# A two-layer transformer on one core: the first attention moves its tokens, outputs are normalised on GpSimd

## The chip, the cores and the metric

One core of one Trainium2 chip. The time is that of the whole launch on the device, in microseconds (us). The engines are named PE (TensorE), PEld (its weight loads), DVE (VectorE), ACT (ScalarE), POOL (GpSimd) and SP (SyncE, here only the queue that issues the DMAs).

## The reference

Two layers over 2048 tokens of width 512, all in fp32. Each layer normalises its input once and adds an attention and a feed-forward of it to the stream.

```python
x = x + attention0(xn) + ffn0(xn)     # 16 heads of 32, block-wise decayed linear attention; top 4 of 16 experts' blocks
xn = layernorm(x)
x = x + attention1(xn) + ffn1(xn)     # 32 heads of 64 over 8 key heads, causal softmax; fp4 weights, silu gate, rms norm
...
h = einsum('nf,ibf->nib', xf, W1b)            # ffn0: 16 blocks of 128 hidden units
h = gelu(h) * mask[:, :, None]
y = einsum('nib,fib->nf', h, W2b)
...
scores = where(causal, einsum('bhqd,bhkd->bhqk', q, kf) / sqrt(64), min)   # attention1
out = einsum('bhqk,bhkd->bhqd', softmax(scores), v)
return out.transpose(0, 2, 1, 3).reshape(b, s, 2048) @ o_w.T
```

## The kernel before

Six stages follow each other, each a block of five engine programs with a barrier at its end: attention0, feed_forward0, projections1, attention1, output1, feed_forward1. Inside a stage the engines are ordered by semaphores alone, written out by hand. All DMAs that matter are issued by SP, in the order of its program. To keep fp32 accuracy, most products are split: each operand is a high part (rounded by ACT) and a low part (the rest, by DVE or GpSimd), and `split_matmul` (lines 50 to 52) makes three matmuls: high by high, high by low, low by high.

**attention0** goes over four chunks of 512 tokens. Its tensors `x`, `xb` and `xn` hold a chunk of tokens, the copy that the output is added to, and the normalised chunk. `xacc` (16 tiles of 128x512), the token stream, is allocated only after this stage.

**feed_forward0** goes over four quarters of four hidden blocks (`q`), in each over four chunks (`c`). For a chunk PE makes four hidden blocks (`HB[b]`, 12 matmuls each), ACT applies gelu, DVE the mask, ACT takes the high part `hT[0]`, GpSimd the low part `hT[1]`, and PE adds the second product into `YB[t]`, 12 matmuls for each of four blocks. In quarters 1 to 3 DVE also unpacks fp4 weights for the last stage between these steps. The first quarter's weights go straight into two rooms of `xacc`, tiles 8 to 15 (`load_first`).

**attention1** has 16 units (key head by sequence) of 24 steps: 16 long ones (queries 512 to 1023) and 8 short ones (queries 0 to 511). In a step PE makes scores (line 1755), DVE the negative maximum (lines 1692, 1695), ACT the exponentials with their sum (line 1662), and DVE transposes them 32 by 32 (lines 1710 to 1715). PE multiplies them with the values in blocks of 32 keys (line 1770) at later steps: `SHORT_VALUES` and `LONG_VALUES` give, for a step counted from the unit's first, the blocks, so that steps from 24 on fall into the next unit. ACT evicts finished halves at the steps of `SHORT_LEFT` and `LONG_LEFT`, and SP stores them to `OT`. At step `INVERT` DVE takes the reciprocals of the sums (line 1721), transposes them (line 1724), and SP writes them to `R`. Within `attention1` GpSimd does nothing.

**output1** goes over 32 steps (2 sequences of 16 pairs of heads). Each loads a row of `OT` into `of` and its reciprocals from `R`, spread over 64 partitions each, into `rd`; DVE multiplies them (line 1921), ACT and GpSimd make the parts (lines 1895, 1902), PE does 24 matmuls. In the first 16 steps a slice of `WoG` is loaded and split too. Row 0, its reciprocals and two slices are loaded ahead at the end of attention1 (`output1_rooms`).

## Time and profile before

| | us |
|---|---|
| median of 3 runs | 2274.7 |
| lowest, highest | 2269.36, 2278.79 |
| profiled execution, its time | 2273.54 |
| its span (first to last instruction) | 2271.8 |
| PE, DVE, ACT, POOL busy in it | 2084.5, 1578.6, 845.8, 366.6 |
| mean granted TensorE clock | 0.964 of 2.4 GHz |

The span is what the rows below count from; the time of the execution is 1.7 us more. PE is busy in 92% of the span, but this share is a mean over stages with different limits.

### The profile page before, as it was taken

How to read it: one execution, taken by the hardware profiler on the slowest of the kernel's cores; microseconds unless marked ns; L12 is line 12 of the kernel's file. 1: busy time of each engine (PE TensorE's matmuls, PEld its weight loads, DVE VectorE, ACT ScalarE, POOL GpSimd, SP SyncE). 2: the span in 40 equal slices, each digit the busy share in tenths (PEclk: the TensorE clock that was granted, in tenths of full speed). 3: DMA queues.
4: the chain of work that ended last, by engine and by line, in shares of the span. 5: the costliest groups of instructions: out<-in, count | busy, mean ns of one | idle time of the engine just before them, and what ended most of it. 6: DMA issues, size and time to landing. Idle time of an engine off the chain costs nothing. (4 is left out here: it accounts for less than half of the span.)

```text
span 2271.8 us, 52890 instructions
## 1 busy us (share of the span) xinstructions
PE 2084.5 (92%) x21680; PEld 1472.5 (65%) x21680; DVE 1578.6 (69%) x2439; ACT 845.8 (37%) x1773; POOL 366.6 (16%) x249
## 2 busy tenths in 40 slices
PE   7999969999998999978998898998988899999998
PEld 5777748887786788734444444444445687787776
DVE  5544323699976345499989999999994462577776
ACT  4322122222223200055555655556553221234443
POOL 0111111323220155400000000000000344221111
PEclk9999989999998999979999999999998899999999
DMA  5122145344427633423333433333332999420101
GB/s 182 57 94 76 38 172 181 102 132 132 125 76 285 184 111 125 150 67 103 100 91 96 116 101 97 104 94 104 110 92 78 286 249 273 141 84 19 56 1 38
DMA packets 205019, 268.18 MB, mean 118 GB/s; under 512 B 42304, under 2 KB 123520, under 8 KB 202112
## 3 DMA queue, kind: packets, MB, share of 16 engines
q1 hardware_dynamic: 203936, 264.85, 38.4%
q8 instruction: 162, 2.65, 0.5%
q14 instruction: 57, 0.47, 0.1%
q10 hardware_dynamic: 864, 0.21, 0.0%
HBM read 181.81 MB, written 83.17 MB: 117 GB/s over the span
## 5 line engine op out<-in xcount | busy, mean ns | idle before, releaser
L1662 ACT ACTIVATE a_prob<-ps,a_nmax 128x256 f32<-128x256 f32 (+7 forms) x512 | 376.7, 738 | 326.9 <-DVE a_nmax L1692 228.7
L1755 PE MATMUL ps<-xacc 64*128 64x512 f32 (+5 forms) x1536 | 389.7, 550 | 80.8 <-ACT a_prob L1662 74.9
L1692 DVE TENSOR_REDUCE a_nmax<-ps 128x1 f32<-128x1024 f32 (+3 forms) x256 | 256.2, 1001 | 45.8 <-PE ps L1755 44.7
L1755 PEld LDWEIGHTS ps<-xacc 64*128 64x128 f32 x1536 | 146.4, 197 | 200.1 <-ACT a_prob L1662 118.4
L1713 DVE STREAM_TRANSPOSE a_pt_long<-a_prob 128x768 f32<-128x768 f32 (+1 forms) x256 | 238.0, 930 | 0.0
L2083 DVE SCALAR_TENSOR_TENSOR f_part<-ps,f_gu_scale,f_part 128x512 f32<-128x512 f32 x264 | 185.2, 746 | 66.9 <-PE ps L2130 53.5
L1770 PE MATMUL ps<-a_pt_long,xacc 32*64 32x256 f32 (+2 forms) x6144 | 211.7, 386 | 1.3 <-ACT a_o L1672 1.3
L1770 PEld LDWEIGHTS ps<-a_pt_long,xacc 32*64 32x64 f32 x6144 | 122.4, 137 | 109.5 <-issue 97.9
L940 POOL TENSOR_TENSOR f_hT_lo<-f_h,f_hT_hi 128x512 fp32r<-128x512 f32 x64 | 93.8, 1474 | 286.4 <-ACT f_hT_hi L923 286.4
L1902 POOL TENSOR_TENSOR o_oT_lo<-xacc,o_oT_hi 128x512 fp32r<-128x512 f32 x2 | 2.9, 1497 | 803.7 <-ACT o_oT_hi L1895 803.7
L1752 PE MATMUL ps<-xacc 64*128 64x128 bf16 x1024 | 113.8, 227 | 5.2 <-ACT a_prob L1662 5.0
L50 PE MATMUL ps<-o_wo_hi,o_oT_hi 128*128 128x512 f32 x256 | 103.2, 403 | 16.6 <-POOL o_oT_lo L1902 16.2
L1695 DVE TENSOR_REDUCE a_nmax<-ps 128x2 f32<-128x1024 f32 (+3 forms) x128 | 105.4, 823 | 17.0 <-PE ps L1755 15.0
L50 PE MATMUL ps<-f_xt_hi,f_w_hi 128*128 x256 | 100.6, 393 | 17.7 <-DMA f_xt_lo<-scratch_xt 17.7
L1710 DVE STREAM_TRANSPOSE a_pt_short<-a_prob 128x512 f32<-128x512 f32 (+3 forms) x256 | 114.1, 484 | 0.0
L1770 PEld LDWEIGHTS ps<-a_pt_short,xacc 32*64 32x64 f32 x3712 | 71.8, 134 | 60.6 <-issue 45.3
L1368 DVE TENSOR_TENSOR k_rp<-ps,k_cosq 128x512 f32<-128x512 f32 x64 | 43.9, 686 | 94.0 <-POOL k_qo L1245 78.7
L919 ACT ACTIVATE f_gl<-ps 128x512 f32<-128x512 f32 x64 | 38.1, 595 | 183.5 <-PE ps L52 183.5
L1245 POOL TENSOR_TENSOR k_qo<-k_rp 128x512 f32<-128x512 f32 x64 | 87.4, 1386 | 102.6 <-DVE k_rp L1368 102.6
L50 PE MATMUL ps<-f_w_hi,f_hT_hi 128*128 128x512 f32 x256 | 101.1, 395 | 2.9 <-POOL f_hT_lo L940 2.4
L51 PE MATMUL ps<-o_wo_lo,o_oT_hi 128*128 128x512 f32 x256 | 101.4, 396 | 0.0
L52 PE MATMUL ps<-o_wo_hi,o_oT_lo 128*128 128x512 f32 x256 | 101.2, 395 | 0.0
(234 smaller groups left out, 4489.7 us busy)
## 6 DMA issues: line engine op xcount, KB each, us to landing
xacc<-scratch_QT SPq DMA_DIRECT2D x512, 64.0 KB, 2.0
scratch_QT<-k_qo SPq DMA_DIRECT2D x64, 256.0 KB, 2.3
xacc<-scratch_V SPq DMA_DIRECT2D x64, 256.0 KB, 4.7
scratch_OT<-a_o SPq DMA_DIRECT2D x32, 512.0 KB, 5.0
o_of<-scratch_OT SPq DMA_DIRECT2D x31, 512.0 KB, 5.2
o_rd<-scratch_R SPq DMA_DIRECT2D x62, 256.0 KB, 8.0
f_block<-in_packed SPq DMA_DIRECT2D x33, 256.0 KB, 3.6
f_mask<-scratch_maskT SPq DMA_DIRECT2D x16, 512.0 KB, 5.1
```

What stands on the lines that cost most here:

```text
L50: pe.matmul(out, lh[lsel], rh[rsel], start=first, stop=False)
L51: pe.matmul(out, lh[lsel], rl[rsel], start=False, stop=False)
L52: return pe.matmul(out, ll[lsel], rh[rsel], start=False, stop=last)
L1662: last = nc.scalar.activation(prob[:, n % PRING, s].rearrange("p (a w) -> p a w", w=w), SC[n % 2][:, a, 0:w], ACT.Exp, bias=nmax[:, n % 4, ...
L1692: nc.vector.tensor_reduce(nmax[:, n % 4, 0:1], SC[n % 2][:, :, 0:width(0, t)], AX.XY, ALU.max, negate=True).then_inc(maxed, 1)
L1695: nc.vector.tensor_reduce(nmax[:, n % 4, :], SC[n % 2][:, :, 0:width(1, t)], AX.X, ALU.max, negate=True).then_inc(maxed, 1)
L1710: last = nc.vector.transpose(pt_short[:, 0:blocks, h, t, :], src)
L1713: last = nc.vector.transpose(pt_long[:, unit % 2, 0:near, h, t - 4, :], src[:, 0:near, :])
L1752: pe.matmul(sc[:, a, w - P:w], identb[r, s, :], causal[r, s, :], start=s == 0, stop=False, skip_group_check=True)
L1755: last = pe.matmul(sc[:, a, 0:w], q[r, slot, heads[a * hf], :], kt[r, b, keys], start=not masked, stop=True, skip_group_check=True)
L1770: last = pe.matmul(out[:, :, a - t0:4, :], v[rows, b, j, :], part[rows, c::2, a - p0:t0 + 4 - p0, :], start=j == 0, stop=j == BLOCKS[hf] - ...
L2083: nc.vector.scalar_tensor_tensor(part[:, s % 2, i, :], PB[(2 * k + i) % 4], gu_scale[:, s % NBK, i, k:k + 1], part[:, s % 2, i, :], ALU.mu ...
```

## The change

It has five parts.

1. `xacc` is allocated before attention0, which keeps `xb`, `xn` and `x` in its tiles 0 to 3, 8 to 11 and 12 to 15. In its last chunk, when `xn` and `x` are used up, SP loads the first quarter's W1T and W2T into their rooms.
2. feed_forward0 begins with four loads: the first and second half of the first chunk's k, high and low part each. PE's first hidden block waits for the halves by themselves (`first_xt`). The first chunk has a loop of its own on PE.
3. In the second product of feed_forward0 PE does, for a hidden block, the eight matmuls with `hT[0]` first (waiting for `h_hi`), and then the four with `hT[1]` (waiting for `h_lo`).
4. In attention1 the short value blocks go in another order over six steps in place of five, their eviction and both stores move by a step, `INVERT` is one step earlier, and each finished half is multiplied with its reciprocals there, by GpSimd for 31 halves and by DVE for the last. The reciprocals come back from `R` by two DMAs a half (`load_inverse`), into one buffer.
5. output1 loads rows already normalised: no `rd`, no multiplication; rows 0 and 1 are loaded ahead.

```diff
@@ attention0, SP
+                    else:
+                        sp.wait_ge(xt_done, KC * NCH)
+                        for dst, src in zip(feed_forward0_rooms(xacc), (d["W1T"][:, 0:C], d["W2T"][0:C, :])):
+                            sp.dma_start(dst, src.rearrange("(k p) n -> p k n", p=P)).then_inc(rest_in, 16)
...
@@ attention0, tensors
-        x = sb("x", [P, TPC, C])
-        xb = sb("xb", [P, TPC, C])
-        xn = sb("xn", [P, TPC, C])
+        xb, xn, x = [xacc[:, r * TPC:(r + 1) * TPC, :] for r in (0, 2, 3)]
...
@@ feed_forward0, SP
-                load_first(0, d["W1T"][:, 0:QC])
+                xt_in.give_credit(sp)
+                for i in range(2):
+                    for s in range(2):
+                        sp.dma_start(xt[s][:, 2 * i:2 * i + 2, 0:CH].bitcast(F32), d["xt"][s][:, 2 * i:2 * i + 2, 0:CH]
+                                     ).then_inc(first_xt[i].sem, 16)
...
-                load_chunk(0)
-                load_first(1, d["W2T"][0:QC, :])
...
@@ feed_forward0, PE
+                                if first and b == 0 and k % 2 == 0:
+                                    pe.wait_ge(first_xt[k // 2].sem, 32)
...
-                            pe.wait_ge(h_lo.sem, h_lo.now(it, b + 1))
+                            pe.wait_ge(h_hi.sem, h_hi.now(it, b + 1))
                             for t in range(TPC):
...
-                                last = split_matmul(pe, YB[t], hT, [w[:, p] for w in w2], b == 0, b == BPQ - 1,
-                                                    np.s_[:, b, t * P:(t + 1) * P], np.s_[:, b, :])
+                                part = hT[0][:, b, t * P:(t + 1) * P]
+                                for s in range(2):
+                                    pe.matmul(YB[t], part, w2[s][:, p, b, :], start=b == 0 and s == 0, stop=False)
+                            pe.wait_ge(h_lo.sem, h_lo.now(it, b + 1))
+                            for t in range(TPC):
+                                last = pe.matmul(YB[t], hT[1][:, b, t * P:(t + 1) * P], w2[0][:, p, b, :],
+                                                 start=False, stop=b == BPQ - 1)
...
@@ attention1
-SHORT_VALUES = {26: range(0, 3), 27: range(3, 6), 28: range(6, 9), 29: range(9, 13), 30: range(13, 16)}
+SHORT_VALUES = {26: (0, 15, 14, 13, 12), 27: (11, 10, 9, 8), 28: (7, 6), 29: (5, 4), 30: (3, 2), 31: (1,)}
...
-SHORT_LEFT = {31: (0,), 32: (1,)}
+SHORT_LEFT = {32: (0, 1)}
...
-SHORT_STORE, LONG_STORE = 34, 50
-INVERT = USTEPS + 2
+SHORT_STORE, LONG_STORE = 35, 51
+SHORT_INVERSE, LONG_INVERSE = 29, 36
+INVERT = USTEPS + 1
...
@@ attention1, SP
-                    sp.wait_ge(evicted, 2 * i + 2)
+                    sp.wait_ge(scaled, i + 1)
...
+                def load_inverse(u, hf):
+                    g, b = divmod(u, NB1)
+                    tok = slice(FIRST[hf] * P, (FIRST[hf] + 4) * P)
+                    sp.wait_ge(r_stored, 64 * (u + 1))
+                    wait(sp, scaled, order(u, hf))
+                    for a in range(2):
+                        sp.dma_start(rd[a * HD1:(a + 1) * HD1, :, :],
+                                     d["R"][g, b, a::2, tok].partition_broadcast(HD1)).then_inc(rd_in, 16)
...
@@ attention1, GpSimd
+                for i in range(2 * NU - 1):
+                    pool.wait_ge(evicted, 2 * i + 2)
+                    pool.wait_ge(rd_in, 32 * (i + 1))
+                    nc.gpsimd.tensor_tensor(o[:, i % 2].rearrange("p s t i q -> p s (t i q)"),
+                                            o[:, i % 2].rearrange("p s t i q -> p s (t i q)"), rd[:], ALU.mult
+                                            ).then_inc(scaled, 1)
...
@@ output1
-                    for a in range(2):
-                        sp.dma_start(rd[a * HD1:(a + 1) * HD1, n % 2, :],
-                                     d["R"][k // 2, b, 2 * (k % 2) + a, :].partition_broadcast(HD1)
-                                     ).then_inc(o_in[n % 3], 16)
...
-                        nc.vector.tensor_tensor(row(n, s), row(n, s), inverse(n, s), ALU.mult).then_inc(scaled, 1)
```

Three places of the order show what moves. The first is SP's queue from the last loads of attention0 to the first of feed_forward0 (`f_xt` is the chunk of normalised tokens, `scratch_x` the output of attention0). Before:

```order
L230 DMA scratch_x<-a_xb 128x512 [waits a0_y_out] x4
L179 UNCONDITIONAL_BRANCH [waits a0_y_stored,a0_mask_stored,a0_xt_stored]
L792 UNCONDITIONAL_BRANCH [waits barrier_Pool_Activation_PE_DVE_SP_release]
L798 DMA xacc<-in_W1T 128x4x512
L809 DMA f_mask<-scratch_maskT 128x4x512
L803 DMA f_xt_hi<-scratch_xt 128x4x512 [waits f0_xt_in]
L803 DMA f_xt_lo<-scratch_xt 128x4x512
L798 DMA xacc<-in_W2T 128x4x512
```

And now:

```order
L227 DMA xacc<-in_W1T 128x4x512 [waits a0_xt_done]
L227 DMA xacc<-in_W2T 128x4x512
L229 DMA scratch_maskT<-a_maskT 16x512 [waits a0_mask_out]
L232 DMA scratch_x<-xacc 128x512 [waits a0_y_out] x4
L177 UNCONDITIONAL_BRANCH [waits a0_y_stored,a0_rest_in,a0_mask_stored,a0_xt_stored]
L800 UNCONDITIONAL_BRANCH [waits barrier_Pool_Activation_PE_DVE_SP_release]
L814 DMA f_xt_hi<-scratch_xt 128x2x512
L814 DMA f_xt_lo<-scratch_xt 128x2x512
L814 DMA f_xt_hi<-scratch_xt 128x2x512
L814 DMA f_xt_lo<-scratch_xt 128x2x512
L818 DMA f_mask<-scratch_maskT 128x4x512
```

Both weight loads stand ahead of the barrier, and the first chunk comes in four loads directly behind it.

The second is PE in feed_forward0, at the start of the second product of a chunk (`f_hT` is the hidden tile, `f_w` the second weights). Before:

```order
L52 MATMUL ps<-f_xt_hi,f_w_lo 128x512
L50 MATMUL ps<-f_w_hi,f_hT_hi 128x512 [waits f0_y_added,f0_h_lo,f0_w_lo]
L51 MATMUL ps<-f_w_lo,f_hT_hi 128x512
L52 MATMUL ps<-f_w_hi,f_hT_lo 128x512
L50 MATMUL ps<-f_w_hi,f_hT_hi 128x512 [waits f0_y_added]
```

And now:

```order
L52 MATMUL ps<-f_xt_hi,f_w_lo 128x512
L1061 MATMUL ps<-f_w_hi,f_hT_hi 128x512 [waits f0_y_added,f0_h_hi,f0_w_lo]
L1061 MATMUL ps<-f_w_lo,f_hT_hi 128x512
L1061 MATMUL ps<-f_w_hi,f_hT_hi 128x512 [waits f0_y_added]
L1061 MATMUL ps<-f_w_lo,f_hT_hi 128x512
L1061 MATMUL ps<-f_w_hi,f_hT_hi 128x512 [waits f0_y_added]
L1061 MATMUL ps<-f_w_lo,f_hT_hi 128x512
L1061 MATMUL ps<-f_w_hi,f_hT_hi 128x512 [waits f0_y_added]
L1061 MATMUL ps<-f_w_lo,f_hT_hi 128x512
L1064 MATMUL ps<-f_w_hi,f_hT_lo 128x512 [waits f0_h_lo]
L1064 MATMUL ps<-f_w_hi,f_hT_lo 128x512 x3
```

The wait for the low part has moved behind eight matmuls that need only the high part.

The third is DVE in attention1 at steps 25 and 26 of a unit (`a_nmax` the maxima, `a_pt` the transposed exponentials, `a_rden` the reciprocals). Before:

```order
L1692 TENSOR_REDUCE a_nmax<-ps 128x1 [waits a1_exped,a1_scored]
L1710 STREAM_TRANSPOSE a_pt_short<-a_prob 128x4x32 [waits a1_exped]
L1710 STREAM_TRANSPOSE a_pt_short<-a_prob 128x4x32
L1692 TENSOR_REDUCE a_nmax<-ps 128x1 [waits a1_exped,a1_scored]
L1713 STREAM_TRANSPOSE a_pt_long<-a_prob 128x24x32 [waits a1_exped]
L1715 STREAM_TRANSPOSE a_pt_wide<-a_prob 128x8x32
L1721 RECIPROCAL a_rden<-a_den 128x32 [waits a1_exped]
L1724 STREAM_TRANSPOSE a_rdenT<-a_rden 128x32 [waits a1_inverted]
L1692 TENSOR_REDUCE a_nmax<-ps 128x1 [waits a1_exped,a1_scored]
```

And now:

```order
L1727 TENSOR_REDUCE a_nmax<-ps 128x1 [waits a1_exped,a1_scored]
L1745 STREAM_TRANSPOSE a_pt_short<-a_prob 128x4x32 [waits a1_exped]
L1745 STREAM_TRANSPOSE a_pt_short<-a_prob 128x4x32
L1756 RECIPROCAL a_rden<-a_den 128x32 [waits a1_exped]
L1759 STREAM_TRANSPOSE a_rdenT<-a_rden 128x32 [waits a1_inverse]
L1727 TENSOR_REDUCE a_nmax<-ps 128x1 [waits a1_exped,a1_scored]
L1748 STREAM_TRANSPOSE a_pt_long<-a_prob 128x24x32 [waits a1_exped]
L1750 STREAM_TRANSPOSE a_pt_wide<-a_prob 128x8x32
```

The reciprocal and its transpose now stand one maximum earlier.

## Rows read from the trace of the kernel before

**Rows 1.** Stretches (windows): busy us of each engine, granted clock, DMA share, GB/s.

```profile
core 0: us, PE busy (x) PEld busy (x) DVE busy (x) ACT busy (x) POOL busy (x), PEclk, DMA share, GB/s
...
309.50:688.30 378.80, 353.75 (x1537) 288.93 (x1537) 272.98 (x405) 99.97 (x168) 93.79 (x64) 0.97 0.44 139
...
964.60:1729.10 764.50, 681.31 (x13354) 355.31 (x13350) 706.83 (x1047) 438.97 (x1078) 0.00 (x0) 0.95 0.35 97
...
1762.50:1957.50 195.00, 182.50 (x768) 145.75 (x768) 85.60 (x65) 42.86 (x49) 77.01 (x33) 0.97 0.90 248
```

**Rows 2.** Timeline, first feed-forward's start: start, us, engine, line, operation [idle before].

```profile
309.50 0.40 SPq L798 DMA_DIRECT2D xacc<-in_W1T  x1
...
314.71 2.19 ACT L911 ACTIVATE f_w_hi<-xacc 128x512 fp32r<-128x512 f32 x4 [23.06 <-DMA xacc<-in_W1T]
...
323.74 0.79 PE L50 MATMUL ps<-f_xt_hi,f_w_hi 128*128 x1 [17.67 <-DMA f_xt_lo<-scratch_xt]
...
328.33 0.39 PE L50 MATMUL ps<-f_xt_hi,f_w_hi 128*128 x1
```

**Rows 3.** First feed-forward: timeline, one chunk as a stretch, timeline at its end.

```profile
511.78 0.50 PE L50 MATMUL ps<-f_w_hi,f_hT_hi 128*128 128x512 f32 x1 [0.49 <-POOL f_hT_lo L940]
...
510.30:533.20 22.90, 22.33 (x98) 17.85 (x97) 20.84 (x32) 5.72 (x11) 6.21 (x4) 1.00 0.44 130
...
678.33 2.73 DVE L1025 TENSOR_TENSOR xacc<-ps,xacc 128x512 f32<-128x512 f32 x4 [7.52 <-PE ps L52]
```

**Rows 4.** Timeline of DVE, second attention: a first period, and one late period.

```profile
964.63 1.22 DVE L1692 TENSOR_REDUCE a_nmax<-ps 128x1 f32<-128x1024 f32 x1 [5.71 <-PE ps L1755]
...
1681.52 1.23 DVE L1692 TENSOR_REDUCE a_nmax<-ps 128x1 f32<-128x1024 f32 x1 [0.32 <-PE ps L1755]
...
1685.33 1.23 DVE L1692 TENSOR_REDUCE a_nmax<-ps 128x1 f32<-128x1024 f32 x1 [0.66 <-PE ps L1755]
...
1687.69 0.31 DVE L1721 RECIPROCAL a_rden<-a_den 128x32 f32<-128x32 f32 x1
...
1688.17 1.18 DVE L1692 TENSOR_REDUCE a_nmax<-ps 128x1 f32<-128x1024 f32 x1
```

**Rows 5.** Timeline of PE, second attention: products of short value blocks.

```profile
1685.22 1.55 PE L1770 MATMUL ps<-a_pt_short,xacc 32*64 32x256 f32 x48
...
1692.22 1.09 PE L1770 MATMUL ps<-a_pt_short,xacc 32*64 32x64 f32 x64
```

**Rows 6.** Stretches, second attention: one whole period, and part of the next.

```profile
1635.01:1681.52 46.51, 41.80 (x883) 22.41 (x883) 44.12 (x66) 27.67 (x69) 0.00 (x0) 1.00 0.37 104
...
1694.90:1702.70 7.80, 5.16 (x30) 1.84 (x30) 7.80 (x13) 5.04 (x10) 0.00 (x0) 0.81 0.13 36
```

**Rows 7.** Timeline of DVE and GpSimd in the output product; a group of the page.

```profile
1763.15 0.69 DVE L1916 TENSOR_TENSOR o_wo_lo<-xacc,o_wo_hi 128x512 fp32r<-128x512 f32 x1 [31.67 <-ACT o_wo_hi L1890]
...
1771.81 2.39 POOL L1902 TENSOR_TENSOR o_oT_lo<-o_of,o_oT_hi 128x1024 fp32r<-128x1024 f32 x1 [3.68 <-ACT o_oT_hi L1895]
...
1772.28 2.47 DVE L1916 TENSOR_TENSOR o_wo_lo<-o_stage,o_wo_hi 128x512 fp32r<-128x512 f32 x1 [1.65 <-ACT o_wo_hi L1890]
...
L1368 DVE TENSOR_TENSOR k_rp<-ps,k_cosq 128x512 f32<-128x512 f32 x64 | 43.9, 686 | 94.0 <-POOL k_qo L1245 78.7
```

**Rows 8.** Timeline, second attention's tail and output product; an issue group of the page.

```profile
1757.78 1.09 ACT L1672 ACTIVATE a_o<-ps 128x512 f32<-128x512 f32 x2 [16.03 <-PE ps L1770]
...
1732.30 2.70 SPq L1609 DMA_DIRECT2D scratch_R<-a_rdenT  x4
...
1766.59 0.76 PE L50 MATMUL ps<-o_wo_hi,o_oT_hi 128*128 128x512 f32 x1 [8.85 <-POOL o_oT_lo L1902]
...
1956.20 0.39 PE L51 MATMUL ps<-o_wo_lo,o_oT_hi 128*128 128x512 f32 x1
...
1956.43 0.39 PE L52 MATMUL ps<-o_wo_hi,o_oT_lo 128*128 128x512 f32 x1
...
o_rd<-scratch_R SPq DMA_DIRECT2D x62, 256.0 KB, 8.0
```

More of the change, by code:

```diff
@@ L724, with feed_forward0_rooms @@
 NF = NCH * NBK
+def feed_forward0_rooms(xacc):
+    return [xacc[:, T // P - (2 - j) * KC:T // P - (1 - j) * KC, :] for j in range(2)]
 def feed_forward0(nc, ps, d, xacc):
@@ L1028, in _ @@
             def _(pe):
-                for q in range(NQ):
+                for q, c0, c1 in ((0, 0, 1), (0, 1, NCH), *((q, 0, NCH) for q in range(1, NQ))):
                     p = q % 2
-                    with pe.Fori(0, NCH) as c:
+                    first = q == 0 and c0 == 0
+                    with pe.Fori(c0, c1) as c:
                         it = c + q * NCH
-                        if q == 0:
+                        if q == 0 and not first:
                             pe.wait_ge(xt_in.sem, xt_in.now(c, 32))
@@ L1652, in exponents @@
                     if n % USTEPS == 0:
-                        wait(act, inverted, unit - 1)
+                        wait(act, inverse, 2 * (unit - 1))
                     act.wait_ge(maxed, n + 1)
@@ L1797, in output1_rooms @@
     stage = xacc[:, 0:2, :]
-    of, rd = [xacc[:, r:r + 2, :].rearrange("p r n -> p (r n)") for r in (3, 5)]
-    return stage, of, rd
+    rows = [xacc[:, r:r + 2, :].rearrange("p r n -> p (r n)") for r in (3, 5)]
+    return stage, rows
 def output1(nc, ps, d, xacc, early):
```

79 lines of the change are left out of this document (41 added, 38 removed).

## The prediction

> **What bounds the kernel now.** I read the profile by stage first, then the start, one period and the end of each stage that the change touches. The stage view [rows 1] has three rows to look at. In the first feed-forward (309.5 to 688.3 us) PE is busy 353.8 of 378.8 us. In the second attention (964.6 to 1729.1) DVE is busy 706.8 of 764.5 us, PE 681.3, and GpSimd has nothing at all. In its output product (1762.5 to 1957.5) PE is busy 182.5 of 195.0, and the DMA share is 0.90, the highest of the three, while DVE and ACT idle more than half. So the bound is PE, then DVE with PE just behind it, then PE with the DMA engines just behind it. Every microsecond that the change takes from such a stage is worth one at the end, since the stages are parted by barriers.
>
> **First feed-forward, its start.** Before, W1T is issued at 309.50 us and ACT can split it from 314.71 on, and PE's first product waits for the low half of the first token chunk, which lands only at 323.74: 17.67 us idle [rows 2]. The first block of hidden units is through when the second begins, at 328.33. The change has both weight tensors in place, so ACT splits at once (2.19 us a tensor, so W1 is ready some 3 us after the barrier), and the queue holds token data alone. W1T shows that 1 MB landed 5.2 us after its issue. The first two quarter loads are also 1 MB together, issued within a microsecond, and should land near 315.4. The other 1 MB I put 4 us later, 319.4 (before, 3.5 MB took 14.2 us, so 4 us a MB). PE then does six products in 2.6 us, waits to 319.4, does six more (at the slow pace of a cold start, 0.43 us each) and is at the second block at 322.0. That is 328.3 - 322.0 = 6.3; I take **-6.5**, as the clock may rise in the second half. Bounds: -4 (the mask, x1 and the next chunk, now issued without waiting, share the engines: two more MB by 4 us each would eat half) and -9 (all 2 MB at the pace of W1T).
>
> **Its steady chunks.** In the quarters with unpacking, PE stands still at the first product with the hidden tile: 0.49 us of waiting on GpSimd's low part at 511.78 [rows 3]; the view of waits has five of these. The new order needs only the high part there and the low part eight matmuls (1.8 us) later. But a chunk in this stretch takes 22.9 us of which DVE is busy 20.8 [rows 3], and the rest of DVE's time there is a wait for the split of the next weights. DVE sets the period; the later wait gives PE some lead once, it does not shorten the period. I take **-1.5** (one lead), bounds 0 and -6 (each of six chunks 1.1 us shorter). The last chunk pays: the four outputs now finish within 0.7 us of each other rather than 0.7 us apart, and DVE's four adds (2.73 us [rows 3]) come almost wholly after them. **+1.2**, bounds 0 and +2. The W1T and W2T loads at the end of the first attention, and the token tensors' new place, cost nothing: PE sets that stage and the queue is nearly idle in it; uncovered they would be the 5 us of one MB twice, in a stage whose last 50 us have no other large load but x.
>
> **Second attention, the reciprocal.** Steps are paced by DVE: maximum, then transposes. In the period that begins at 1681.52 DVE idles 0.66 us before the third maximum, at 1685.33, and one step later spends 1687.69 to 1688.17, 0.48 us, on the reciprocal and its transpose [rows 4]. The change issues them one step earlier, into the idle place. 15 times 0.48 is **-7**. It needs PE's next scores 0.5 us earlier as well; those stand behind the first short value blocks, 1.55 us for three wide blocks [rows 5]. The new first portion is one wide block (a third, 0.52) and four narrow ones. The row at 1692.22 has 64 narrow products in 1.09 us, so 40 cost 0.68: 1.2 in all, 0.35 less. That just suffices. Bounds 0 (PE late) and -7.2.
>
> **Second attention, the clock.** From 964.63 to 1681.52 there are 15 periods, 47.8 us each [rows 4], yet a period without a fall of the clock takes 46.51 [rows 6]. Together the excess is 19.2 us. In the row for 1694.90 to 1702.70 the granted clock averages 0.81, between the two levels of 2.4 and 1.2 GHz; in the part of the period just there PE has scores only, the last short block being done and the long ones not begun, and is busy 5.2 of 7.8 us. The reversed order spreads the short blocks over one more step and so shortens this lean stretch from three steps to somewhat over two. I expect about half of the falls to go: **-10**, bounds 0 and -19. This is the least certain term.
>
> **The multiplications.** 31 of 32 go to GpSimd, which is idle there; each is 128x1024, the shape of the 2.39 us row [rows 7]. They lie between steps 32 and 35 and between 47 and 50 of a period, with their inverse rows loaded from step 29 and about 36 on; an 8.0 us landing [rows 8] is four steps, which fits. SP now waits for `scaled` ahead of query loads, but it gets there only after the scores of step 12 of the next period, some 6 us after the eviction. The added wait is met by then, and query loads keep their lead of several steps. The same 16 MB of inverse rows (62 loads of 256 KB before) move from a stage with DMA share 0.90 to one with 0.35 [rows 1]. What it costs DVE is the open point. [rows 7] show DVE's SBUF product taking 0.69 us alone and 2.47 us when it met GpSimd at work (1771.81 to 1774.20): it ended 0.55 after GpSimd did, so it was held for 1.78. But 64 products with one input from PSUM, issued beside GpSimd's rotation, average 686 ns, nothing lost. DVE's work in the attention is of neither kind exactly: maxima read PSUM, transposes read one SBUF operand. Bounds: 0 and 31 x 1.78 = 55 us. I take 0, since the held operation has two SBUF inputs and the transposes have one. The Trainium skill (SBUF — State Buffer, Who interferes with whom) states that the port pair is an exclusive lock, taken by a DVE instruction with two SBUF inputs or in a two-port mode, and not by one with a single SBUF input outside these modes. By its lock rule taken for every DVE operation the term would be the upper bound, by its exception the lower; the two rows above agree with both halves, and no row here shows a transpose beside GpSimd.
>
> **The tail.** The last long half goes to DVE after the eviction (1757.78 + 1.09), before the final store: +1.2. The output product then starts without its first multiplication (0.64 us a half) and its signal, about -1.2: PE's first product came 4.1 us after the stage began (1766.59 [rows 8]). The chain of the last unit's inverse rows must be ready: R is issued to 1735.0, then 8.0 (load) + 2.4 (GpSimd) + 8.0 (load) end at 1753.4, which leaves 5 us for R's landing and the issues ahead. Sum **0**, bounds -1 and +6.
>
> **The output product.** 768 matmuls from 1766.59 to 1956.43 plus one pace, 190.1 us; at the pace of the last two, 0.23 (0.2275 over longer stretches), they need 174.7. Of the 15.4 us over, some 2.3 is the cold start (the first eleven at 0.43), which stays. The rest is waiting for rows behind saturated DMA engines, and the clock's fall after one such wait. Without the inverse loads the traffic of the stage shrinks by 62 x 256 KB = 16 MB of about 48 MB (248 GB/s times 195 us [rows 1]), so 32 MB are left, 165 GB/s. **-12.5**, bounds -7 and -13.
>
> **Sum.** -6.5 - 1.5 + 1.2 - 7 - 10 + 0 - 12.5 = -36.3. The profiled execution took 2273.5 us (span 2271.8 and 1.7 around it), 1.2 below the median of the three runs, 2274.7. Forecast **2237**.
>
> **Rivals.**
> - *The second attention gains nothing* (PE's scores come no earlier, the clock falls as often). For it: PE is busy 681 of 764 us, so the reciprocal's idle place is partly PE's; the falls may move instead of vanish. Against: 0.66 of idle is there in every period. 2273.5 - 6.8 - 12.5 = **2254**. Chance 0.18.
> - *GpSimd holds DVE's transposes* in the second attention. Place: DVE between maxima. At 1.78 us for each of 31, less what falls on a maximum, I reckon 1.65 x 31 = 51: 2237 + 51 = **2288**, slower. It decides the sign from 36.3 / 31 = 1.2 us an operation. For it: the 2.47 us row. Against: the PSUM rows. Chance 0.10.
> - *SP's order binds*: the wait for R's landing or for `scaled` holds back query, K or V loads, 2 us a period, 30 us in all: **2267**, no change that can be told. Against: queries are fetched steps ahead. Chance 0.06.
> - The forecast case, 2224 to 2250: 0.66.
>
> **How the numbers follow.** Half a per cent of 2274.7 is 11.4 us, about what can be told from no change: faster means below 2263.3. The forecast case and the first rival are faster (0.84), with 0.02 of the third; the second rival has 0.08 slower and 0.02 same; the third 0.04 same: faster 0.86, same 0.06, slower 0.08. The range 2220 to 2262 holds the forecast case with nearly all clock falls gone at its low end, and the first rival with a poorer start at its high end; about 0.17 is left out above and below.
>
> **What the changed profile would show.** PE's first feed-forward product near 315.5 with a short second wait; no wait of PE on GpSimd's low part with 0.5 us; the stage 6 to 7 us shorter. In the second attention no idle of 0.66 before the third maximum, GpSimd products of 2.4 us, transposes of unchanged length beside them, fewer slow stretches of clock, some 747 us in place of 764.5. In the output product DMA share near 0.65 and no idle of PE after the start. Wrong would be: transposes of 2 to 3 us; PE waiting for the second half of the tokens past 322; a clock row of 0.93 in every second period still; a last load of inverse rows that ends after the last eviction.

## The result, and the profile after

The changed kernel takes 2234.2 us (median of 4 runs, 2232.9 to 2236.4), the kernel before 2276.7 beside it (4 runs): ratio 0.9824, 95% interval 0.9801 to 0.9847. The forecast was 2237. The profiled execution after took 2236.4 us, with a span of 2234.7, 37.1 below the 2271.8 of before. The differences in this section are between these two executions.

The view by stretches, of the three stages that [rows 1] shows for before, then one chunk of the first feed-forward, and two periods of the second attention, the second with a fall of the clock:

```profile
core 0: us, PE busy (x) PEld busy (x) DVE busy (x) ACT busy (x) POOL busy (x), PEclk, DMA share, GB/s
307.84:678.12 370.28, 352.63 (x1537) 289.15 (x1537) 271.75 (x405) 99.92 (x168) 94.16 (x64) 0.98 0.43 136
955.30:1705.00 749.70, 676.26 (x13355) 347.53 (x13350) 706.95 (x1049) 438.79 (x1079) 68.33 (x29) 0.97 0.45 119
1740.38:1920.90 180.52, 177.13 (x768) 146.12 (x768) 43.97 (x32) 42.23 (x49) 77.99 (x33) 0.98 0.51 175
...
523.72:546.55 22.83, 22.13 (x96) 17.83 (x96) 20.77 (x32) 5.64 (x11) 6.23 (x4) 1.00 0.39 127
...
1423.83:1470.00 46.17, 42.05 (x883) 22.07 (x883) 44.17 (x66) 27.64 (x69) 4.71 (x2) 1.00 0.47 128
1470.00:1517.60 47.60, 43.55 (x883) 22.52 (x883) 44.48 (x66) 27.66 (x69) 4.71 (x2) 0.96 0.48 124
```

The feed-forward lost 8.5 us, the attention 14.8, the output product 14.5, and the number of PE's products in them is the same (13355 for 13354 records in the attention). In the output product the DMA share went from 0.90 to 0.51 and DVE's work halved; in the attention GpSimd now works and the DMA share rose from 0.35 to 0.45, while DVE's busy time stayed at 707 us. The granted clock rose in each stage.

The timeline at the first feed-forward's start (answers to [rows 2]):

```profile
307.67 4.27 ACT L916 ACTIVATE f_w_hi<-xacc 128x512 fp32r<-128x512 f32 x8 [17.81 <-PEq L177]
307.84 0.40 SPq L814 DMA_DIRECT2D f_xt_hi<-scratch_xt  x1
308.33 4.91 DVE L999 TENSOR_TENSOR f_w_lo<-xacc,f_w_hi 128x512 fp32r<-128x512 f32 x8 [3.33 <-ACT f_w_hi L916]
313.34 0.76 PE L50 MATMUL ps<-f_xt_hi,f_w_hi 128*128 128x512 f32 x1 [9.07 <-DVE f_w_lo L999]
316.04 0.29 PEld L50 LDWEIGHTS ps<-f_xt_hi,f_w_hi 128*128 128x128 f32 x1 [0.53 <-DMA f_xt_lo<-scratch_xt]
316.63 0.63 PE L51 MATMUL ps<-f_xt_lo,f_w_hi 128*128 128x512 f32 x1
318.77 0.44 PE L50 MATMUL ps<-f_xt_hi,f_w_hi 128*128 128x512 f32 x1
```

ACT and DVE split at the barrier. PE begins 5.50 us after SP's first issue instead of 14.23, has its seventh weight load released by the landing of the second half, at 316.04, which costs it 0.16 us (the eighth product comes 0.59 us after the seventh, at 316.04 too, instead of 0.43), and is at the second hidden block after 10.93 us instead of 18.83. The releaser in brackets at 313.34 is not what PE waited for: it needs four of DVE's eight low parts, W1's, and these were done at 310.8. The loads of the first half had landed at 313.20, 0.14 us before the product.

PE and DVE further on in that stage: PE at the turn of a chunk (its product before begins at 522.63), PE's waits over 307 to 668 us, and DVE's adds at the end (answers to [rows 3]):

```profile
523.72 0.50 PE L1061 MATMUL ps<-f_w_hi,f_hT_hi 128*128 128x512 f32 x1 [0.70 <-ACT f_hT_hi L928]
```
The wait there, by the view of waits (us in total, times, longest):
```profile
PE ps L1061 <- ACT f_hT_hi L928: 3.1, 4, 0.8
```
By the timeline:
```profile
668.43 2.48 DVE L1030 TENSOR_TENSOR xacc<-ps,xacc 128x512 f32<-128x512 f32 x4 [8.88 <-PE ps L1064]
```

The wait for GpSimd's low part is gone, and a wait for ACT's high part stands in its place, longer and four times instead of five. The chunk is 22.83 us, as before within 0.1, with DVE busy 20.77.

DVE at the start of a quick period of the second attention, and the maxima of positions 37 and 38 (answers to [rows 4]):

```profile
1423.83 1.22 DVE L1727 TENSOR_REDUCE a_nmax<-ps 128x1 f32<-128x1024 f32 x1 [0.32 <-PE ps L1797]
1424.97 0.49 DVE L1745 STREAM_TRANSPOSE a_pt_short<-a_prob 128x128 f32<-128x128 f32 x2
...
1426.50 0.49 DVE L1745 STREAM_TRANSPOSE a_pt_short<-a_prob 128x128 f32<-128x128 f32 x2
1426.91 0.31 DVE L1756 RECIPROCAL a_rden<-a_den 128x32 f32<-128x32 f32 x1
...
1427.64 1.23 DVE L1727 TENSOR_REDUCE a_nmax<-ps 128x1 f32<-128x1024 f32 x1 [0.17 <-PE ps L1797]
...
1430.00 1.19 DVE L1727 TENSOR_REDUCE a_nmax<-ps 128x1 f32<-128x1024 f32 x1
...
1449.66 0.82 DVE L1727 TENSOR_REDUCE a_nmax<-ps 128x1 f32<-128x640 f32 x1
1451.52 0.83 DVE L1727 TENSOR_REDUCE a_nmax<-ps 128x1 f32<-128x640 f32 x1 [0.15 <-PE ps L1797]
```
GpSimd's timeline in that period, and the evictions of the short half (ACT) with the long half's first products (PE):
```profile
1424.73 2.35 POOL L1716 TENSOR_TENSOR a_o<-a_o,a_rd 128x1024 f32<-128x1024 f32 x1 [24.76 <-ACT a_o L1698]
...
1442.63 1.07 ACT L1698 ACTIVATE a_o<-ps 128x512 f32<-128x512 f32 x2
...
1443.85 1.12 PE L1812 MATMUL ps<-a_pt_long,xacc 32*64 32x256 f32 x32
```

The reciprocal fills what was idle: 0.17 us is left of 0.66, and the step after it takes 2.36 us instead of 2.84 (1427.64 to 1430.00; before 1685.33 to 1688.17). GpSimd works from 1424.73 to 1427.08, across four transposes, two maxima and the reciprocal, and none of them is longer than elsewhere. At 1449.66 a step takes 1.86 us that took 1.72 before. The text on the change says that the short half's eviction moves by a step; in fact only the first of its two evictions does, so that both now stand at position 32, one behind the other, and the first product of the long half begins 0.15 us after their end.

The tail and the start of the output product (answers to [rows 8]):

```profile
1734.49 1.08 ACT L1698 ACTIVATE a_o<-ps 128x512 f32<-128x512 f32 x2 [18.29 <-PE ps L1812]
1735.61 1.23 DVE L1772 TENSOR_TENSOR a_o<-a_o,a_rd 128x1024 f32<-128x1024 f32 x1 [28.73 <-ACT a_o L1698]
...
1743.04 0.76 PE L50 MATMUL ps<-o_wo_hi,o_oT_hi 128*128 128x512 f32 x1 [8.59 <-POOL o_oT_lo L1934]
```
Groups of the page after:
```profile
L1748 DVE STREAM_TRANSPOSE a_pt_long<-a_prob 128x768 f32<-128x768 f32 (+1 forms) x256 | 237.8, 929 | 0.0
L1716 POOL TENSOR_TENSOR a_o<-a_o,a_rd 128x1024 f32<-128x1024 f32 x31 | 73.0, 2356 | 696.3 <-ACT a_o L1698 686.3
```
By the page's DMA issues (count, KB each, us to landing):
```profile
a_rd<-scratch_R SPq DMA_DIRECT2D x64, 256.0 KB, 4.4
...
o_of<-scratch_OT SPq DMA_DIRECT2D x30, 512.0 KB, 4.0
```

**Where the 37.1 us came from**, by the starts of the same instruction in both traces (periods are counted between the first maxima of units; the quick period is the usual one without a fall of the clock, and "over the quick period" is what 15 of them took beyond 15 times that, mostly falls, but other pauses too):

| from, to | before | after | difference |
|---|---|---|---|
| start, SP's first issue of the first feed-forward | 309.5 | 307.8 | -1.7 |
| to PE's second hidden block | 18.8 | 10.9 | -7.9 |
| to its last product | 351.6 | 349.9 | -1.7 |
| to the projections' first product | 8.3 | 9.4 | +1.1 |
| to unit 0's first maximum | 276.4 | 277.2 | +0.9 |
| to unit 15's first maximum | 716.9 | 702.9 | -13.9 |
| ... of it 15 quick periods | 15 x 46.51 | 15 x 46.17 | -5.1 |
| ... of it over the quick period | 19.2 | 10.4 | -8.9 |
| to the output product's first product | 85.1 | 84.7 | -0.3 |
| to its last | 189.8 | 176.7 | -13.1 |
| to the end | 315.3 | 314.9 | -0.5 |

### The profile page after: what moved, and what is told of

Same layout as the page of the kernel before. It is cut to its first block and busy times, and to the rows that moved or that the text cites. A ratio compares the mean times of both kernels' runs of the same rounds, so it can differ in the third digit from the quotient of the medians.

```text
span 2234.7 us, 52900 instructions
## 1 busy us (share of the span) xinstructions
PE 2069.3 (93%) x21680; PEld 1461.3 (65%) x21680; DVE 1536.4 (69%) x2407; ACT 844.8 (38%) x1773; POOL 441.3 (20%) x280
## 5 line engine op out<-in xcount | busy, mean ns | idle before, releaser
L1797 PE MATMUL ps<-xacc 64*128 64x512 f32 (+5 forms) x1536 | 382.5, 540 | 69.5 <-ACT a_prob L1688 63.2
L1812 PE MATMUL ps<-a_pt_long,xacc 32*64 32x256 f32 (+1 forms) x6144 | 206.7, 377 | 6.0 <-issue 3.9
L1716 POOL TENSOR_TENSOR a_o<-a_o,a_rd 128x1024 f32<-128x1024 f32 x31 | 73.0, 2356 | 696.3 <-ACT a_o L1698 686.3
L945 POOL TENSOR_TENSOR f_hT_lo<-f_h,f_hT_hi 128x512 fp32r<-128x512 f32 x64 | 94.2, 1480 | 276.6 <-ACT f_hT_hi L928 276.6
L1812 PEld LDWEIGHTS ps<-a_pt_short,xacc 32*64 32x64 f32 x3712 | 65.0, 134 | 71.8 <-issue 55.6
L50 PE MATMUL ps<-f_xt_hi,f_w_hi 128*128 (+1 forms) x256 | 100.9, 394 | 9.1 <-DVE f_w_lo L999 9.1
L2100 POOL TENSOR_TENSOR f_hT_lo<-f_h,f_hT_hi 128x512 fp32r<-128x512 f32 x44 | 57.6, 1309 | 255.7 <-ACT f_hT_hi L2056 255.7
L1812 PE MATMUL ps<-a_pt_short,xacc 32*64 32x192 f32 (+3 forms) x3712 | 99.0, 307 | 5.6 <-issue 3.1
```

The lines of the kernel that those rows point to most:

```text
L50: pe.matmul(out, lh[lsel], rh[rsel], start=first, stop=False)
L1797: last = pe.matmul(sc[:, a, 0:w], q[r, slot, heads[a * hf], :], kt[r, b, keys], start=not masked, stop=True, skip_group_check=True)
L1812: last = pe.matmul(out[:, :, a - t0:4, :], v[rows, b, j, :], part[rows, c::2, a - p0:t0 + 4 - p0, :], start=j == 0, stop=j == (LONG_LAST, ...
```

## The experiments

Each kernel is the changed one with one edit, if nothing else is said. Numbers of stages are from each run's trace, by the same markers as in the table above. The median of the changed kernel and its ratio, 0.9824, are from other runs than these, so a difference of ratios below 0.004 says little, and the traces decide.

**The reciprocal one step later again.**
```
-INVERT = USTEPS + 1
+INVERT = USTEPS + 2
```


> The changed kernel with the reciprocal and its transpose one step later (step position 18 instead of 17), where they stood before; all else as changed, the output is the same. Theory (the softmax maximum of a step waits for the exponential of the step before it, and the reciprocal in front of it made VectorE late for the whole period): first to last maximum of the units gets longer by 15 x 0.33 to 0.48, so +5 to +7 us, with the idle time ahead of the maximum that follows the inverse near 0.66 us again and the stages outside the first attention within 1 us. Rival (the period is set by TensorE, and what was gained came from the clock alone): within 1.5 us of the changed kernel.


Measured: 2240.5 us, ratio 0.9853 [0.9823, 0.9883], against 0.9824 some 6.6 us. The same steps of DVE in a quick period, and that period:
```profile
1435.54 1.22 DVE L1727 TENSOR_REDUCE a_nmax<-ps 128x1 f32<-128x1024 f32 x1 [0.66 <-PE ps L1797]
...
1438.38 1.18 DVE L1727 TENSOR_REDUCE a_nmax<-ps 128x1 f32<-128x1024 f32 x1
```
As a stretch:
```profile
1431.73:1478.38 46.65, 42.20 (x883) 22.07 (x883) 44.16 (x66) 27.65 (x69) 4.71 (x2) 1.00 0.47 127
```
The idle 0.66 us is back and the quick period is 0.48 longer, 46.65 us; 15 periods took 711.9 for 702.9, of which 1.7 us is over the quick period. The theory stands, though this trace, of the slowest of five executions, is longer than expected in the attention (9.0 us for 5 to 7) and by 1.8 us between its last unit and the output product. The period is also 0.14 *longer* than before the change, although the reciprocal stands where it stood: something else in the change costs 0.14 us.

**The short half spread as before.**
```
+SHORT_VALUES = {26: range(0, 3), 27: range(3, 6), 28: range(6, 9), 29: range(9, 13), 30: range(13, 16)}
+SHORT_LAST, LONG_LAST = 15, 31
```


> The changed kernel with the value products of the short half spread in ascending order over the step positions 26 to 30 again, as before (the eviction stays at 32); the output is the same. Theory (the dense packing at 26 and 27 keeps TensorE from the idle stretch in which its granted clock fell to the lower level, at the cost of a fuller step position there): falls of double length, near 6.8 us, come back and the first attention gets longer by 5 to 10 us against the changed kernel. Rival (the falls go with the reciprocal's stall or with the phase of the steps, not with these products): within 1.5 us, falls still single ones of 3.4 us.


Measured: 2244.0 us, ratio 0.9870 [0.9841, 0.9898], about +10. 15 periods took 713.5 us, 10.5 more. In the 14 periods after the first the clock falls ten times, for four in the changed kernel's trace. One of these periods:
```profile
1429.75:1477.64 47.89, 43.29 (x883) 22.86 (x883) 44.59 (x66) 27.66 (x69) 4.71 (x2) 0.96 0.45 124
```
By the timeline:
```profile
1450.84 0.92 DVE L1727 TENSOR_REDUCE a_nmax<-ps 128x1 f32<-128x768 f32 x1
1453.56 0.96 DVE L1727 TENSOR_REDUCE a_nmax<-ps 128x1 f32<-128x768 f32 x1 [0.93 <-PE ps L1797]
```
A step of 2.72 us (1.72 in a quick period) shows the fall, and the falls cost 1.4 us each; those of double length, which were expected, did not come back. The quick period is 46.47: 0.30 of the gain of 0.48 is gone too, at the two steps behind the reciprocal (2.62 and 2.36 us for 2.36 and 2.32), where PE brings the scores too late. So the order of the short half carries both gains, which I had seen for the clock alone.

**The old order of products in the first feed-forward.** Each token tile takes `split_matmul`'s three products again, after `h_lo`.


> The changed kernel with the old order of the products in the first feed-forward's second half (each token tile takes its three partial products at once, after the low half of the hidden values is ready); the same sums in another order. Theory (VectorE's adds and splits set the chunk's period, TensorE's wait is only what is left over): the middle chunks together +1.5 to +2 us, the gap after the last chunk -1.1 us, in sum 0 to +1.5 us. Rival (TensorE's waits for the low half are the chunk's bound, 16 chunks less one at 0.4 us): +5 to +7 us.


Measured: 2234.8 us, ratio 0.9827 [0.9797, 0.9857]. From the second hidden block to the last product +1.6 us, gap at the end -1.1, in sum +0.5; PE's wait for GpSimd's low part is there again, five times, 2.3 us in all. The theory stands: DVE sets the chunk, and the new order is worth half a microsecond.

**Waiting for the whole first chunk.**
```
-if first and b == 0 and k % 2 == 0:
-    pe.wait_ge(first_xt[k // 2].sem, 32)
+if first and b == 0 and k == 0:
+    pe.wait_ge(first_xt[0].sem, 32)
+    pe.wait_ge(first_xt[1].sem, 32)
```


> The changed kernel, in which the first product of the first feed-forward waits for both halves of its first chunk of tokens instead of the first half; weights come early as changed; the output is the same. Theory (the gain of the start is the weights', which no longer stand ahead of the tokens; the two halves land close together): 0 to +1.5 us. Rival (the halves carried the larger part of the start's gain): +3 to +5 us.


Measured: 2238.7 us, ratio 0.9841 [0.9810, 0.9872]. PE begins 8.27 us after SP's first issue (5.50 in the changed kernel) and is at the second block after 13.52 (10.93):
```profile
317.83 0.77 PE L50 MATMUL ps<-f_xt_hi,f_w_hi 128*128 128x512 f32 x1 [11.84 <-DMA f_xt_lo<-scratch_xt]
...
323.08 0.63 PE L50 MATMUL ps<-f_xt_hi,f_w_hi 128*128 128x512 f32 x1
```
That is +2.6 us, between the two expectations: of the 7.9 us of the start a third is the halves', and the rest is the new queue's, that is the weights in place and the tokens first, which no run takes apart. The feed-forward also starts 1.7 us later in this trace, behind the first attention, which the edit did not touch.

**The multiplications on DVE.** The 31 products move from GpSimd's block to DVE's loop, at step positions 34 and 49.


> The changed kernel with the 31 multiplications of the first attention on VectorE instead of GpSimd, queued at step positions 34 and 49 of each unit behind the transposes; the output is the same. Theory (VectorE sets the period, so its own work counts in full, while GpSimd's lies beside it): 31 x 1.23 us = +38 us less what falls into idle time or clock falls, so +25 to +38 us. Rival (VectorE has enough idle time in the steps that TensorE bounds): under +10 us.


Measured: 2247.8 us, ratio 0.9885 [0.9870, 0.9901], +13.9 us. Less than the theory, more than the rival. The group, and one of the periods, which take 47.75 us in 12 of 15 cases:
```profile
L1749 DVE TENSOR_TENSOR a_o<-a_o,a_rd 128x1024 f32<-128x1024 f32 x32 | 38.0, 1188 | 26.1 <-ACT a_o L1698 14.5 <-DMA a_rd<-scratch_R 11.6
```
As a stretch:
```profile
1481.53:1529.28 47.75, 42.35 (x883) 22.10 (x883) 46.15 (x68) 27.65 (x69) 0.00 (x0) 1.00 0.46 123
```
The quick period is 1.58 us longer, 23.7 in all, less than the 2.38 of two multiplications because the steps behind have less idle time. But after the first period the clock no longer falls: 15 periods are 716.6 us, within 0.4 of 15 times 47.75, so 10 us come back. The expectation took the period for the whole and forgot the clock's share. Against the same work on DVE at these two places, the move to GpSimd is worth 14 us.

**More work on GpSimd.** Behind each of the 31, three of
```
+nc.gpsimd.tensor_tensor(idle[:], idle[:], idle[:], ALU.mult).then_inc(scaled, 1)
```


> The changed kernel with three more 128x512 multiplications on GpSimd, of a tile of ones that nothing reads, behind each of the 31; the output is the same. Theory (GpSimd's elementwise work in this stage does not hold up VectorE's reductions and transposes, whose mean is unchanged while the 31 run): mean durations of VectorE's instructions unchanged and the time within 1.5 us. Rival (each such operation takes VectorE's transposes or the DMA issues with it, as at the multiplication at 1771.81 before the change, where both engines took 2.4 us instead of 1.23): 93 x 0.3 to 1.2 us, +28 to +110 us.


Measured: 2237.8 us, ratio 0.9848 [0.9828, 0.9867]; in the trace the span is 2233.8 and the 15 periods 702.3 us (702.9). A group of the page:
```profile
L1754 DVE STREAM_TRANSPOSE a_pt_long<-a_prob 128x768 f32<-128x768 f32 (+1 forms) x256 | 237.9, 929 | 0.0
```
97 us more of GpSimd's work in the stage leave the mean of DVE's long transposes as it was, 929 ns, and that of the short half's at 485. The theory stands for the durations, and the rival's 28 us are excluded. The median is 2 us above its bound, with runs from 2233.9 to 2241.8; the trace shows no stage for that. The expectation misreads the row at 1771.81: 2.39 us is GpSimd's ordinary time for 128x1024 (2356 ns on average), and what was held there is DVE's 128x512, 2.47 us for 0.69. The Trainium skill (SBUF — State Buffer, Who interferes with whom) states that a DVE instruction with one SBUF input outside the two-port modes does not take the lock that shuts GpSimd out; this run agrees for the transposes, which have one such input.

**The inverse rows' transfers again.** In the output product, after each load of attention rows:
```
+for a in range(2):
+    sp.dma_start(spare[a * HD1:(a + 1) * HD1, n % 3, :],
+                 d["R"][k // 2, b, 2 * (k % 2) + a, 0:SEQ - 32].partition_broadcast(HD1)).then_inc(o_in[n % 3], 16)
...
-                            act.wait_ge(o_in[n % 3], 16 * (n // 3 + (1 if n % 3 == 2 else 0)))
+                            act.wait_ge(o_in[n % 3], 48 * (n // 3 + (1 if n % 3 == 2 else 0)))
```
ACT now waits for all three loads of a step, as DVE did before the change.


> The changed kernel in which the output product loads 992 of the 1024 columns of the inverse rows again for each of its steps, into a tile that nothing reads; no multiplication by them; the output is the same. Theory A (the transfers of these rows, which stood among the loads of the attention's rows, made TensorE wait in the output product): +9 to +13 us from its first to its last product. Theory B (the multiplications and their place ahead of the splits did): within 2 us.


Measured: 2249.8 us, ratio 0.9894 [0.9878, 0.9910], +15.9. The stage as a stretch, PE's waits in it, and the landing of the transfers:
```profile
1747.50:1942.50 195.00, 184.92 (x768) 148.52 (x768) 36.87 (x32) 43.11 (x49) 77.65 (x33) 0.96 0.92 240
```
The wait there, by the view of waits (us in total, times, longest):
```profile
PE ps L50 <- POOL o_oT_lo L1939: 15.3, 4, 8.6
```
By the page's DMA issues (count, KB each, us to landing):
```profile
o_of<-scratch_OT SPq DMA_DIRECT2D x30, 512.0 KB, 8.2
o_spare<-scratch_R SPq DMA_DIRECT2D x60, 248.0 KB, 10.0
```
191.3 us from the first to the last product, 14.5 more (somewhat over the 9 to 13 expected), although nothing is multiplied. PE waits three times more, 6.7 us, and is busy 7.8 us longer at a granted clock of 0.96 for 0.98. The rows of the attention land after 8.2 us instead of 4.0, but the inverse rows, which ACT waits for here, come later still, after 10.0; the kernel before landed the attention's rows after 5.2 us and the inverse rows after 8.0 (medians of its page), and DVE waited 74.8 us for the latter. Theory A stands: the transfers and the wait for them account for the whole gain of the stage, 13.1 us, and the multiplications on DVE cost nothing there that can be told. This trace, of the slowest of four executions, is also 6.4 us longer in the second attention, whose code is the changed kernel's; see the clock below.

**The long half early.**
```
+SHORT_VALUES = {26: (0, 15, 14, 13, 12), 27: (11, 10, 9, 8), 28: (7, 6, 5), 29: (4, 3), 30: (2, 1)}
+LONG_VALUES = {33: range(0, 2), 34: range(2, 4), 35: range(4, 6), 36: range(6, 8), 37: range(8, 10), 38: range(10, 11),
+               39: range(11, 12), 40: range(12, 14), 41: range(14, 15), 42: range(15, 18), 43: range(18, 21), ...
+SHORT_LEFT = {31: (0, 1)}
```


> The changed kernel with the short half's value products over the step positions 26 to 30 only, its evictions at 31, and the long half's from 33 instead of 34, so that positions 38, 39 and 41 carry one block less; the output is the same. Theory (the remaining falls of the clock come after the lean positions 31 to 34, and the steps at 37 and 38 are bound by TensorE because the long half starts late): fewer of the 6 falls and up to 0.14 us less in each period, -2 to -12 us. Rival (VectorE sets the steps and the falls move elsewhere): within 2 us.


Measured: 2225.9 us, ratio 0.9796 [0.9783, 0.9809], -8.3 us against the changed kernel's median, -6.4 by the ratios. The quick period is 45.64 us; the longer ones still have a low clock:
```profile
1416.80:1463.87 47.07, 43.50 (x883) 22.46 (x884) 44.38 (x67) 27.61 (x69) 4.71 (x2) 0.96 0.47 126
1463.87:1509.51 45.64, 42.00 (x883) 22.06 (x883) 44.00 (x67) 27.59 (x69) 4.72 (x2) 1.00 0.49 128
```
0.53 us a period, 8.0 in all, is more than I allowed for, since the steps at positions 38 to 42, too, wait less for PE. The time over the quick period, 11.8 us, is no smaller than the changed kernel's 10.4. So the gain is right in size and wrong in one of its two reasons.

**The reciprocal alone.** The kernel *before*, with `INVERT = USTEPS + 1` and nothing else.


> The kernel before with the reciprocal and its transpose one step earlier, and nothing else of the change; the output is the same. Theory now (the value products spread evenly over positions 26 to 30 make TensorE late at the step that follows the reciprocal, so only 0.18 us of the 0.48 us comes out of each period, as the pair of runs on the inverse and on the short half suggests, and without the later eviction nothing is given back): quick periods of 46.33 us for 46.51, -2.7 us, and falls of the clock as before. Rival (each edit keeps its own gain): quick periods of 46.03 us, -7.2 us.


Measured: 2275.9 us against 2274.5 (12 and 17 runs), ratio 1.0003 [0.9978, 1.0027]: nothing that can be told, with an interval of some 5.6 us to either side. In its trace DVE waits a second time behind the reciprocal, and 14 of 15 periods are longer than 47.8 us; after the first the clock falls 13 times, most often at one place:
```profile
1354.80 1.23 DVE L1692 TENSOR_REDUCE a_nmax<-ps 128x1 f32<-128x1024 f32 x1 [0.17 <-PE ps L1755]
1357.41 1.23 DVE L1692 TENSOR_REDUCE a_nmax<-ps 128x1 f32<-128x1024 f32 x1 [0.18 <-PE ps L1755]
```
As a stretch:
```profile
1350.99:1398.87 47.88, 43.28 (x883) 22.93 (x883) 44.59 (x66) 27.66 (x69) 0.00 (x0) 0.96 0.38 102
1366.00:1376.50 10.50, 8.25 (x94) 3.64 (x94) 9.57 (x15) 6.08 (x13) 0.00 (x0) 0.84 0.13 37
```
The step takes 2.62 us for 2.84 and the next 2.36 for 2.32, -0.18 as expected; a period without a fall, which this trace has not, would be 46.33 us. 15 of these leave 27.0 us over, for 19.2 before. The stretch between the short and the long half's products then ends in a fall nearly every time.

**The evictions one step apart.** `30: (3, 2, 1)` for `30: (3, 2), 31: (1,)`, and `SHORT_LEFT = {31: (0,), 32: (1,)}`.


> The changed kernel with the short half's last value product at step position 30 and its two evictions at 31 and 32 as before, the long half from 34 as changed; the output is the same. Theory (TensorE waits at 34 for the two evictions that the change put together at 32, and brings 0.14 us of that to the steps at 37 and 38): the gap of 1.72 us at the maximum of position 38 is back for 1.86, quick periods of 46.04 us for 46.18, -2 us. Rival (the evictions are done in time; the 0.14 us is from elsewhere): quick periods of 46.18 us.


Measured: 2228.6 us, ratio 0.9812 [0.9773, 0.9851], with runs from 2221 to 2242. DVE's maxima of positions 37 and 38, a quick period, and the longest one:
```profile
1447.62 0.79 DVE L1727 TENSOR_REDUCE a_nmax<-ps 128x1 f32<-128x640 f32 x1
1449.34 0.82 DVE L1727 TENSOR_REDUCE a_nmax<-ps 128x1 f32<-128x640 f32 x1
```
As a stretch:
```profile
1375.77:1421.79 46.02, 41.75 (x883) 22.17 (x883) 44.11 (x66) 27.67 (x69) 4.70 (x2) 1.00 0.49 129
1513.85:1566.19 52.34, 47.08 (x883) 24.16 (x883) 44.98 (x66) 27.67 (x69) 4.72 (x2) 0.90 0.42 113
```
The step is 1.72 us again (1447.62 to 1449.34) and the quick period 46.03. The edit also moves block 1 from 31 to 30, but in the run with the short half spread, whose last block stands at 30 too and whose evictions are both at 32, the step is 1.86: the 0.14 us are the evictions'. One period of 52.34 us with a granted clock of 0.90 took the gain away in this execution. It begins with a pause of PE of 1.31 us between scores, in which it waited for nothing that the profile shows. The changed kernel has such a pause of 0.7 us in the same period, the run with the long half early one of 1.3 us; why is open.

**With the last hidden block in the old order.** The long half early, and in the first feed-forward `split_matmul` for the block `b == BPQ - 1` of each chunk.


> The long half early as in the run of that name, and the last hidden block of the first feed-forward's second product in the old order (three products of a token tile at once), so that the adds of the last chunk can start earlier; the other blocks as changed. Theory: the first feed-forward's end gap 1.1 us shorter and its chunks as changed, so -1 us against the run with the long half early, near 2225 us. Rival (the old order's waits in each chunk come back): +1 us.


Measured: 2223.1 us, ratio 0.9786 [0.9756, 0.9817], the lowest of all. But the reason is not the one expected: the gap at the end is 1.1 us shorter and the chunks before it 1.1 us longer, since PE waits five times, 4.1 us, for GpSimd's low part. Both theories are half right, and the sum is 0. The 3 us against the run with the long half early, whose attention is the same, come in the traces from that attention, 692.8 us for 696.5, with low clock in 23.8 us of it for 40.9: a difference between executions, not the edit's.

**The short half's end heavier.** `28: (7, 6), 29: (5, 4), 30: (3, 2, 1)` on the kernel just above; it has the old order of the last hidden block too, which the expectation leaves out, so it is to be held against that run.


> The long half early, with the short half's blocks 7 and 6 at step position 28, 5 and 4 at 29, and 3, 2 and 1 at 30, so that the lean stretch that follows is shorter; the output is the same. Theory (falls follow the emptiest stretch of TensorE, near 1.4 us at the steps of 31 and 32): a fall or two fewer, -1 to -3 us against the run with the long half early. Rival (the falls depend on the phase of the units, not on one stretch): within 1.5 us.


Measured: 2224.4 us, ratio 0.9792 [0.9761, 0.9823]; quick period 45.65 us as there, 10.1 us over it for 8.2. No effect that can be told: the time agrees with the rival.

## Why the prediction was right

The sum was -36.3 and came out as -37.1. That they are this close is partly luck: the start and the part outside the sum brought 1.4 and 1.3 us more than forecast, the reciprocal and the clock 1.9 and 1.1 less. By terms:

- **The start**, -6.5: measured -7.9. The first product came 5.5 us after SP's first issue, forecast 5.9, but the second half had landed by 316.0, 8.2 us after it, for 9.9. The wait for it that the forecast put at over a microsecond was 0.16 us. The pace of "4 us a MB" was the mean of a queue of 3.5 MB; here the second MB landed 2.8 us after the first.
- **The steady chunks and the end of the stage**, -1.5 and +1.2: measured -1.7 and +1.1. The old order alone gives +1.6 and -1.1, while PE's waits for the low part come back. DVE sets the period, as forecast: were it PE's waits, the old order would have cost 5 to 7 us.
- **The reciprocal**, -7: measured -5.1. The step behind it gained the 0.48 us forecast, but 0.14 us a period was given back in the step at position 37. The step that failed is one the working lacks: the change also puts both short evictions at 32, and the long half's first products at 34 wait for them. With them one step apart the quick period is 46.03 us and the 0.48 us are gained in full. My condition, that PE's scores must come earlier and that the new order "just suffices" for it, was right: without that order the reciprocal alone gave 0.18 us a period and nothing in the time that can be told.
- **The clock**, -10: measured -8.9, in a range from 0 to -19. The size is right, the mechanism given for it is not borne out. The working said that the reversed order shortens the lean stretch, the time with scores only between the last short block and the first long one, and that the falls go with its length. The traces (products of PE, record of the granted clock) give, in us:

  | run | lean stretch in a quick period | time at low clock in the 14 periods after the first |
  |---|---|---|
  | before | 7.0 | 41.0 |
  | reciprocal alone (old order) | no quick period | 51.2 |
  | short half spread (old order) | 7.0 | 34.1 |
  | changed kernel | 5.4 | 13.7 |
  | reciprocal one step later | 5.4 | 20.5 |
  | evictions one step apart | 6.5 | 17.1 |
  | long half early | 4.6 | 10.2 |
  | multiplications on DVE | 5.4 | 0.0 |

  So in these traces the new order of the short half halves the time at low clock, or better, with the reciprocal at either place. But with the evictions one step apart the short half ends at 30 and the long one begins at 34, as before; the stretch is nearly as long as it was, and the falls stay few. And with the multiplications on DVE they are gone at an unchanged 5.4 us. The length of the stretch does not decide alone; what in the order does stays open. The size is also one execution's: of four more traces with the changed kernel's attention work on PE and DVE, three have 13.7 us of low clock too (the old order in the first feed-forward, the whole first chunk, more work on GpSimd), and the one with the inverse rows again has 27.3, with 16.8 us over the quick period for 10.4. Against the old order that is more than the 16.4 us of the short half spread, so single traces are thin evidence; but all five executions with the short half spread took 2241 to 2248 us, and the changed kernel's four 2233 to 2236, and the longer quick period makes up 4.5 us of that.
- **The multiplications' cost to DVE**, 0 of 0 to 55: measured 0, also with 97 us of further work beside it. This excludes the rival of 2288 us.
- **The tail**, 0: measured -0.3. DVE's 1.23 us is there, and PE starts 2.7 us after the stage's first issue instead of 4.1.
- **The output product**, -12.5: measured -13.1, and by the run with the transfers alone this is the doing of the transfers and of the wait for them. PE has no wait after its first product but is slowed at times by the clock (granted 0.98). DMA share 0.51, not 0.65, at 175 GB/s for the 165 worked out: the share fell more than the bytes.
- **Not in the sum**: -1.7 up to the first feed-forward and +0.9 - 0.5 elsewhere. Over the twelve traces with the changed first attention, that first time is 307.7 to 309.6 us, mean 308.5; over the two with the old one 309.5 and 310.5. The spread is as large as the 1.7 us, and whether a part of it is the change's stays open. That the weight loads cost the first attention nothing agrees with it.

Of the rivals, SP's order did not bind: in the attention neither PE nor DVE has a wait for a load in the views of waits, and the quick period fell. That the attention gains nothing is what the reciprocal alone would have done.

## What to carry to other kernels

An idle place on the engine that sets the period is worth filling only if what it waits for can come earlier too: move the work into the idle place and lighten what stands ahead of its releaser, or little comes of it. Take large transfers of small data (here an inverse broadcast to 64 partitions, 16 MB) out of the stage whose DMA engines are full, even when their arithmetic is free there. When two evictions are moved together, look at who waits for their bank next.

## What was not expected

- In these runs the granted clock does not go by how quick a period is. 2.4 us more of DVE work a period (the multiplications on DVE), with the same products of PE, ended all falls after the first period, and the reciprocal alone, which made each period quicker, brought one in nearly every period. What decides this stays open.
- Though DVE sets the period, a fall of PE's clock is not hidden behind it: it lengthens a period by 1.4 us after the change (47.60 for 46.17), and by 2.5 before it.
- The rows of the attention (512 KB each) land after 4.0 us at a DMA share of 0.51 and after 8.2 at 0.92, but in the kernel before after 5.2 at 0.90: the share alone does not give the landing time.
